# A graph layer on one core: additions of attention in pairs, a division moved from GpSimd to VectorE, and one-hots cut in four

## The reference

```
h = relu(layernorm(x))                       # node stage
h = h @ W.T                                  # 8 heads of 32
enc = relu(edge_attr @ edge_W.T + edge_b)
alpha = leaky(h[src].a_src + h[dst].a_dst + sum(enc * h[dst]))   # per edge and head
attn = softmax of alpha over the edges of one dst
x = x + segment_sum(h[src] * attn, dst) + bias
h = relu(layernorm(x))                       # second dense stage ("mid")
y1 = relu(batch_norm(gcn_conv(h, W1)))       # conv: sum over edges of table[src], scaled
y2 = relu(batch_norm(gcn_conv(y1, W2)))
x = x + relu(concat(h, y1, y2) @ Wfc + bfc)
```

## Time and profile before

| | us |
|---|---|
| median of 3 runs | 6951.39 (6950.96 to 6955.41) |
| profiled execution, its span | 6959.5 |
| of it: units 0 to 127, node stage 127 to 314 | 314 |
| attention, 314 to 2614 | 2300 |
| second dense stage, 2614 to 2808 | 194 |
| first convolution, 2808 to 4814 | 2006 |
| turn, 4814 to 4890 | 76 |
| second convolution, 4890 to 6872 | 1982 |
| last turn, 6872 to 6959 | 87 |

### The profile page before, as it was taken

The page is one execution under the profiler, slowest core; times in us unless marked ns, Lnnn a source line. Parts: engine busy times, 40 slices in busy tenths (PEclk is TensorE's granted clock), DMA queues, the critical chain, the costliest instruction groups (busy, mean ns, idle before and its releaser), DMA issues. The chain is left out here.

```text
span 6959.5 us, 113181 instructions
## 1 busy us (share of the span) xinstructions
PE 4805.8 (69%) x27409; PEld 3529.7 (51%) x27410; DVE 3523.0 (51%) x8745; ACT 2073.8 (30%) x5831; POOL 4908.5 (71%) x4806
## 2 busy tenths in 40 slices
PE   2699999999999994555555555556666666666655
PEld 1466666666666664344444444445544544444443
DVE  6688888888888888222222222223222222222224
ACT  3567777777777774000000000001000000000001
POOL 1777777776776756677777777774677777777775
PEclk9899999999999997555555555555555555555555
DMA  6777776777776655211111111111211111111115
GB/s 207 250 210 211 210 215 207 211 212 212 212 213 210 209 175 158 82 52 52 51 52 52 51 52 51 52 51 43 53 33 34 34 33 34 34 34 33 33 26 161
DMA packets 515795, 783.25 MB, mean 113 GB/s; under 512 B 143367, under 2 KB 392452, under 8 KB 514956
## 3 DMA queue, kind: packets, MB, share of 16 engines
q0 software_dynamic: 176176, 377.82, 21.0%
q1 hardware_dynamic: 303390, 369.82, 16.6%
q10 hardware_dynamic: 35758, 30.37, 1.4%
HBM read 695.07 MB, written 82.51 MB: 112 GB/s over the span
## 5 line engine op out<-in xcount | busy, mean ns | idle before, releaser
L1690 POOL DMA_INDIRECT c_g<-conv_table,c_idx x3128 | 3010.6, 962 | 1128.3 <-issue 952.9
L1767 PE MATMUL c_sums<-c_g,acc 128*128 x7040 | 1976.1, 441 | 1714.2 <-SPq L1653 1077.4
L1767 PEld LDWEIGHTS c_sums<-c_g,acc 128*128 128x128 f32 x7040 | 1626.4, 322 | 2220.1 <-issue 2210.1
L1002 POOL DMA_INDIRECT acc<-gat_table,ga_idx x1564 | 1615.8, 1033 | 653.0 <-issue 458.2
L1731 DVE TENSOR_TENSOR acc<-acc,c_sums 128x128 f32 (+1 forms) x1760 | 448.5, 255 | 2838.1 <-PE c_sums L1767 2821.7
L1386 PE MATMUL ga_sums<-ga_wg,ga_S 128*128 128x265 f32 x3520 | 999.3, 406 | 7.1 <-DVE ga_wg L1260 6.0
L1336 PE MATMUL ga_dstp<-ga_oht,ga_h 128*128 128x256 bf16 x5280 | 729.9, 275 | 76.0 <-DVE ga_prod L1181 69.7
L1386 PEld LDWEIGHTS ga_sums<-ga_wg,ga_S 128*128 128x128 f32 x3520 | 610.4, 193 | 171.4 <-issue 65.3
L1336 PEld LDWEIGHTS ga_dstp<-ga_oht,ga_h 128*128 128x128 bf16 x5280 | 505.7, 98 | 344.4 <-DVE ga_prod L1181 130.1
L1181 DVE SCALAR_TENSOR_TENSOR ga_prod<-acc,ga_a_dst,ga_dstp 128x512 f32<-128x512 f32 x880 | 645.0, 733 | 8.0 <-issue 6.7
L1077 ACT ACTIVATE ga_S<-iota_row,ga_dcol 128x128 f32<-128x128 f32 x1760 | 605.0, 392 | 73.5 <-issue 70.6
(11 more groups left out here) (253 smaller groups left out, 3731.5 us busy)
## 6 DMA issues: line engine op xcount, KB each, us to landing
ga_h<-h_parts SPq DMA_DIRECT2D x880, 192.0 KB
ga_dl<-dl_rows SPq DMA_DIRECT2D x110, 512.0 KB
c_g<-conv_table,c_idx POOLq DMA_INDIRECT x3128, 2.5
acc<-gat_table,ga_idx POOLq DMA_INDIRECT x1564
h_parts<-h_split SPq DMA_DIRECT2D x14, 1344.0 KB, 5.2
gat_table<-h_out SPq DMA_DIRECT2D x14, 952.0 KB
x_rows<-md_x SPq DMA_DIRECT2D x14, 896.0 KB, 7.1
fc_x<-x_rows ACTq DMA_DIRECT2D x98, 128.0 KB
```

What stands on the lines that cost most here:

```text
L1002: pool.indirect_dma_start(G[:, (v * PC + j) * HROW:(v * PC + j + 1) * HROW], None, gat_table, bass.IndirectOffsetOnAxis(idx[:, c:c + 1], 0 ...
L1690: pool.indirect_dma_start(G[:, c % (2 * SLOTS), :], None, table, bass.IndirectOffsetOnAxis(idx[:, c:c + 1], 0)).then_inc(rows_in[c // 2 % ...
L1767: last = nc.tensor.matmul(sums[:, b % R, 0:width], S[:, u * CH + 2 * b + j, :], flat[:, bass.ds(slots[b] * (2 * width) + j * width, width) ...
```

## The change

Five edits:

1. PE's `slot` in attention goes by steps of two. In each: two additions, then `lines`, `carries`, or `factors` with `turn_back` (now ahead of the quanta), then two quanta, then two dots. DVE, ACT and POOL keep their order there.
2. Rows of counts are loaded into registers as the low 16-bit halves of the same words (`low_halves`).
3. The multiplication of POOL in the second dense stage becomes `share` on DVE: for the first group behind the first reciprocal, for group g+1 at the start of `pre(g)`. POOL keeps the addition of the bias.
4. In `dense_phase` scale and shift are written straight into the tiles that are kept, without the two copies and without the wait for the ReLUs of two groups before; and ACT copies tiles 0 to 5 of a group to `md_hT` instead of 1, 3 and 5.
5. A convolution's one-hots are made by four operations with one tensor input and a scalar per partition, 128 columns each, instead of one of 512 with two tensor inputs.

```diff
--- before.py
+++ after.py
@@ -97,6 +98,12 @@
 def spread(ap, dims):
 
     return AP(ap.tensor, ap.offset, [list(ap.ap[0])] + [list(d) for d in dims])
+
+
+def low_halves(tab):
+
+    halves = tab.bitcast(U16)
+    return AP(halves.tensor, halves.offset, [list(halves.ap[0]), [2, tab.shape[-1]]])
 
 
 def gnn(nc, A, out):
@@ -454,8 +461,9 @@
     mv = sb(ctx, f"{name}_mv", [P, GT, 2])
     var = sb(ctx, f"{name}_var", [P, GT])
     sd = sb(ctx, f"{name}_sd", [P, GT])
-    rstd = [sb(ctx, f"{name}_rstd{u}", [P, GT]) for u in range(2)]
-    shift = [sb(ctx, f"{name}_shift{u}", [P, GT]) for u in range(2)]
+    if keep is None:
+        keep = [sb(ctx, f"{name}_{n}", [P, TILES]) for n in ("rstd", "shift")]
+    rstd, shift = ([t[:, g * GT:(g + 1) * GT] for g in range(GROUPS)] for t in keep)
     if tp is None:
         tp = ps(ctx, f"{name}_tp", [P, NT, 512])
     op = [ps(ctx, f"{name}_op{r}", [P, 512]) for r in range(NO)]
@@ -525,16 +533,10 @@
                 nc.vector.tensor_scalar(var[:, :], mv[:, :, 1], EPS, None, ALU.add).then_inc(s_var, 1)
 
             def normal(g):
-                u = g % 2
                 dve.wait_ge(s_sd, g + 1)
-                if g >= 2:
-                    dve.wait_ge(relu_done, GT * (g - 1))
-                link(nc.vector.reciprocal(rstd[u][:, :], sd[:, :]))
-                nc.vector.scalar_tensor_tensor(shift[u][:, :], mv[:, :, 0], -1.0, rstd[u][:, :], ALU.mult, ALU.mult).then_inc(s_norm, 1)
+                link(nc.vector.reciprocal(rstd[g], sd[:, :]))
+                nc.vector.scalar_tensor_tensor(shift[g], mv[:, :, 0], -1.0, rstd[g], ALU.mult, ALU.mult).then_inc(s_norm, 1)
                 dve.wait_ge(s_norm, g + 1)
-                if keep:
-                    nc.vector.tensor_copy(keep[0][:, g * GT:(g + 1) * GT], rstd[u][:, :])
-                    nc.vector.tensor_copy(keep[1][:, g * GT:(g + 1) * GT], shift[u][:, :])
 
             def copy(n):
                 dve.wait_ge(turn_done, n + 1)
@@ -573,8 +575,8 @@
                     act.wait_ge(s_norm, g + 1)
                 if g >= NH:
                     act.wait_ge(turn_done, GT * (g - NH) + a + 1)
-                nc.scalar.activation(hn[g % NH][:, a, :], xg[g % NX][:, a, :], ACT.Relu, bias=shift[g % 2][:, a:a + 1],
-                                     scale=rstd[g % 2][:, a:a + 1]).then_inc(relu_done, 1)
+                nc.scalar.activation(hn[g % NH][:, a, :], xg[g % NX][:, a, :], ACT.Relu, bias=shift[g][:, a:a + 1],
+                                     scale=rstd[g][:, a:a + 1]).then_inc(relu_done, 1)
 
             def copy(n):
                 act.wait_ge(turn_done, n + 1)
@@ -1050,7 +1052,7 @@
                         act.wait_ge(raw_done, t)
                     take_waits(act, held)
                     return (registers(row_tab[u][0:1, 0, :], mybir.EngineType.Activation, 0, NS - 1),
-                            registers(row_tab[u][0:1, 1, :], mybir.EngineType.Activation, READY + 1, READY + 1 + UNITS // PB))
+                            registers(low_halves(row_tab[u][0:1, 1, :]), mybir.EngineType.Activation, READY + 1, READY + 1 + UNITS // PB))
 
                 def source(regs, b):
 
@@ -1389,25 +1391,27 @@
                 def slot(x, a, b, c, tail, more):
 
                     t, m, v = x.at(), x.at(-1), x.odd(-1)
-                    for k in range(QS):
-                        if k == 0 and tail:
-                            add(x.at(-3), UL - 1)
-                        if k and c:
-                            add(x.at(-2), k - 1)
+                    for k in range(0, QS, 2):
+                        for n in (k - 2, k - 1):
+                            if k == 0 and tail:
+                                add(x.at(-3), UL + n)
+                            if k and c:
+                                add(x.at(-2), n)
                         if b and k == 2:
                             lines(m)
                         if b and k == 4:
                             carries(m, v)
-                        if a and k < QS - 2:
-                            quantum(t, k + 2)
-                        if more and k >= QS - 2:
-                            quantum(t + 1, k + 2 - QS)
-                        if a and k % 2:
-                            dot(t, k - 1)
-                            dot(t, k)
                         if b and k == 6:
                             factors(m)
                             turn_back(m)
+                        for q in (k + 2, k + 3):
+                            if a and q < QS:
+                                quantum(t, q)
+                            if more and q >= QS:
+                                quantum(t + 1, q - QS)
+                        if a:
+                            dot(t, k)
+                            dot(t, k + 1)
                     if a:
                         close(x)
 
@@ -1453,8 +1457,11 @@
             link(nc.vector.tensor_scalar(dens(0, 1), dens(0, 1), 1e-10, None, ALU.max))
             nc.vector.reciprocal(dens(0, 1), dens(0, 1)).then_inc(den_ready, 1)
             nc.vector.tensor_scalar(dinv[:, :], acc[:, :, S0], 1.0, None, ALU.add).then_inc(deg_ready, 1)
+            dve.wait_ge(den_ready, 1)
+            share(dve, 0)
             link(nc.vector.tensor_scalar(dens(1, GROUPS), dens(1, GROUPS), 1e-10, None, ALU.max))
             nc.vector.reciprocal(dens(1, GROUPS), dens(1, GROUPS)).then_inc(den_ready, 1)
+            dve.wait_ge(den_ready, 2)
             dve.wait_ge(root_ready, 1)
             link(nc.vector.reciprocal(dinv[:, :], dinv[:, :]))
             dve.sem_inc(dinv_ready, 1)
@@ -1471,14 +1478,17 @@
             pool.wait_ge(s_w, 32)
             for g in range(GROUPS):
                 heads = columns(g)[:, :, :, 1:HCOLS]
-                den = columns(g)[:, :, :, 0:1]
-                if g < 2:
-                    pool.wait_ge(den_ready, g + 1)
-                nc.gpsimd.tensor_tensor(heads, heads, spread(den, [[WROW, GT], [HCOLS, HEADS], [0, HDIM]]), ALU.mult).then_inc(scaled, 1)
                 pool.wait_ge(scaled, g + 1)
                 nc.gpsimd.tensor_tensor(heads, heads, spread(bias[:, :], [[0, GT], [HDIM, HEADS], [1, HDIM]]), ALU.add).then_inc(attended, 1)
 
+        def share(dve, g):
+
+            heads, den = columns(g)[:, :, :, 1:HCOLS], columns(g)[:, :, :, 0:1]
+            nc.vector.tensor_tensor(heads, heads, spread(den, [[WROW, GT], [HCOLS, HEADS], [0, HDIM]]), ALU.mult).then_inc(scaled, 1)
+
         def pre(dve, g, xg):
+            if g + 1 < GROUPS:
+                share(dve, g + 1)
             dve.wait_ge(attended, g + 1)
             x = xg[:, :, :].rearrange("p t (h d) -> p t h d", d=HDIM)
             nc.vector.tensor_tensor(x, x, columns(g)[:, :, :, 1:HCOLS], ALU.add).then_inc(pre_done, 1)
@@ -1507,7 +1517,7 @@
             nc.scalar.activation(acc1[:, t, :], op[:, 0:F1], ACT.Copy, scale=dinv[:, t:t + 1]).then_inc(done, 1)
 
         dense_phase(nc, sb, ps, sem, held, const, "md", ctx, A["x"], NODES, [w1[:, 0, :], w1[:, 1, :]], F1,
-                    lambda pe: pe.wait_ge(s_w, 32), pre=pre, keep=x1_norm, finish_act=finish_act, by_act=(1, 3, 5), hold=hold, at_end=at_end,
+                    lambda pe: pe.wait_ge(s_w, 32), pre=pre, keep=x1_norm, finish_act=finish_act, by_act=(0, 1, 2, 3, 4, 5), hold=hold, at_end=at_end,
                     reloaded=reloaded, act_before=act_before, sync_before=sync_before, dve_before=dve_before, pool=attend)
 
 
@@ -1600,7 +1610,7 @@
 
 
     _, regs = nc.values_load_multi_w_load_instructions(
-        row, engines=[eng], min_val=USED, max_val=USED + UNITS,
+        low_halves(row), engines=[eng], min_val=USED, max_val=USED + UNITS,
         skip_runtime_bounds_check_because="unit numbers are clamped where they are worked out")
     return regs
 
@@ -1714,8 +1724,10 @@
                     dve.wait_ge(dcol_ready, m + 1)
 
                 def onehots(u, b):
-                    nc.vector.tensor_tensor(S[:, u * CH + 2 * b:u * CH + 2 * b + 4, :], spread(iota_row[:, :], [[0, 4], [1, P]]),
-                                            spread(dcol[u][:, 2 * b:2 * b + 4], [[1, 4], [0, P]]), ALU.is_equal).then_inc(onehot_done, 2)
+                    for c in range(2 * b, 2 * b + 4):
+                        last = nc.vector.tensor_scalar(S[:, u * CH + c, :], iota_row[:, :], dcol[u][:, c:c + 1], None, ALU.is_equal)
+                        if c % 2:
+                            last.then_inc(onehot_done, 1)
 
                 def iteration(m, u, i, fc, more):
                     _, tiles = nc.values_load_multi_w_load_instructions(
@@ -1756,7 +1768,7 @@
                         slot_row[0:1, bass.ds(m * UL, UL)], engines=[mybir.EngineType.PE], min_val=0, max_val=NB * PB - 1,
                         skip_runtime_bounds_check_because="pair numbers are taken modulo the slots where they are worked out")
                     _, needs = nc.values_load_multi_w_load_instructions(
```

(3 more changed lines are left out.)

## The result

The changed kernel takes 7030.8 us in the median of 4 runs (7029.4 to 7033.8), before 6951.2; ratio 1.012, 95% interval 1.0105 to 1.0134. That is slower by 80, inside the range on record (6960 to 7110) and 8 under the forecast of 7039. The parts of the sum fit less well than the sum, and one that was put at nothing measured 52. The stages show where to look.

A forecast was written before the change was run, and what follows sets the result against it. It took PE to bound attention, DVE and POOL blocking each other the second dense stage, and POOL's gathers the convolutions; 6951.4 + 140 (order) − 31 (dense) − 21 (one-hots), loads 0, = 7039 us, range 6960 to 7110.

The forecast's parts named there:

- Attention's order: PE's paired order in attention: DVE's product comes late, net 1.29 us a round over 108 rounds, +140 us (+110 to +175).
- the chain: Attention: first addition of a pair, DVE's flush, weigh and product, then PE's dst; ready at 2.97 us against 2.99.
- k = 0, 2 and 4: Pairs of units in an attention round; product forecast late by 0.76, 0.05 and 1.17 us there.
- Rival B: Attention: the pairs are not late, stalls stay as today; 6899 us, chance 0.08.
- D: Attention: half the stall, only k = 0 and half of k = 4 late; +70, 6969 us, chance 0.07.
- The loads: 16-bit register loads on queues with slack: same number and fields, 0 us, bounds −5 and +5.
- The dense stage: Second dense stage: POOL's multiplication moved to DVE, a group falls from 11.7 to 9.7 us; −31 (−20 to −42).
- rival E: Second dense stage: POOL's addition gets in first, 13.4 us a group; +21 instead of −31, 7091 us, chance 0.07.
- my 8.46: Second dense stage before the change: 8.46 us for a group after POOL's last work, the start of the 9.7 estimate.
- The one-hots: Convolutions: four one-input operations leave 26 of 47 us of gather delay; −21 us, bounds −33 and +15.
- Rival C: Convolutions: one-input one-hots hold POOL's port as a train; +96 instead of −21, 7156 us (spread evenly 7286), chance 0.10.

The follow-up runs named there:

- the base: The kernel before with only the 16-bit register loads (of the row counts) made: 6999.8 us, ratio 1.0074.
- the other edits: The changed kernel with PE's old order put back in attention: 6918.6 us, ratio 0.9955.
- leaky early: The order-only kernel with DVE's leaky and scan moved ahead of the flush at unit 0: 7069.0 us, ratio 1.0171.
- order-only kernel: Also called the order alone: the base with only PE's new order in attention added: 7118.5 us, ratio 1.0247.
- the kernel with 16 halves: The base with ACT's and PE's loads of counts taking 16 contiguous 16-bit halves, the even ones used: 7293.8 us, ratio 1.0493.

## Why the prediction held, term by term

- **Attention's order: right in mechanism, the size left open.** Forecast +140 on the kernel before; measured +119 on the base and +112 beside the other edits, with PE's wait for the product at 144 us in the window where about 170 was named. The places and the waits are those of the chain: 0.76, 0.05 and 1.17 forecast at k = 0, 2 and 4, and 0.70, 0.16 and 1.01 found. Rival B, that the pairs are not late, and D, that they are half as late, are out: leaky early took away just the wait that it should. The order alone also takes in some of the base's own waits for ACT (72 us of them in the window there, 48 in the order-only kernel), so its price without the 16-bit loads may be higher; that was not run.
- **The loads: the step that failed.** The prediction said "The number of register loads is the same, and they fetch the same fields", and put the term at 0. Number and fields are the same, and a load of eight counts takes 1.3 us longer on PE and about 1.2 on ACT. On PE, at 1.93, it is hidden, as the prediction said of queues with slack, and nothing shows a loss from SP's. ACT has slack too, 27% of its time, but the addition came only 0.38 behind the one-hot, and the hole grew by 1.16, from 0.68 to 1.84: +52. What I left out was to bound the duration of an operation that the trace did not show, on each queue, against that queue's lead and not its average.
- **The dense stage: right in mechanism, mis-sized.** Forecast −31, found −46. POOL's addition takes 5.4 behind DVE's (forecast 5.7), never ahead of it, so rival E is out. A group of DVE takes 8.57 (2843.91 to 2852.48 in the timeline below), sometimes 9.14 with a wait for a DMA, where I took 9.7. The timeline of DVE after:

```profile
2843.91 2.03 DVE L1487 TENSOR_TENSOR acc<-acc 128x1792 f32<-128x1792 f32 x1 [0.47 <-DMA md_x<-in_x]
2845.85 2.02 DVE L1494 TENSOR_TENSOR md_x<-md_x,acc 128x1792 f32<-128x1792 f32 x1
...
2850.93 0.49 DVE L533 TENSOR_SCALAR md_var<-md_mv 128x7 f32<-128x7 f32 x1
2851.70 0.20 DVE L537 RECIPROCAL x_scale<-md_sd 128x7 f32<-128x7 f32 x1 [0.27 <-ACT md_sd L571]
...
2852.48 2.02 DVE L1487 TENSOR_TENSOR acc<-acc 128x1792 f32<-128x1792 f32 x1
```

  What is left of the blocking is 0.3 at the variance (0.49, where it takes 0.17 undisturbed). ACT's square root, for which the undisturbed group before waited 1.30, is nearly ready: 0.27. That wait was in my 8.46 and I took no credit for it.
- **The one-hots: right in mechanism, mis-sized.** Forecast −21, found −36 alone, and −36 in the profiles of the changed kernel against the base (4009.1 for 4045.1). Of the term, what remains of the delay was put at 26 between 14 and 62; the mean of 949 over the median of 945 gives 4 × 3128 = 13, the lower bound. The median is 945 in the base too, so that it fell by 2 from the kernel before is not the one-hots' doing. POOL's and DVE's timelines after, one train:

```profile
3507.14 0.98 POOL L1700 DMA_INDIRECT c_g<-conv_table,c_idx  x1 [0.30 <-issue]
```

```profile
3506.63 0.87 DVE L1728 TENSOR_SCALAR acc<-iota_row,c_dcol 128x128 f32<-128x128 f32 x4
```

  The train covers the moment at which the gather reads its indices, 3507.14 + 0.13, and runs on to 3507.50; the gather is late by 0.03 only. Rival C, a port held as a train, would make that 0.23 and is out. The Trainium skill (SBUF — State Buffer, "Who interferes with whom") has a one-input operation in a 2-port mode hold the shared pair for the whole instruction. These runs disagree with a holding as long as the recorded duration. An operation is recorded with 0.28 in the median, the train covers the moment of reading in 735 gathers of the changed kernel, and these have a mean of 959 and none is over 1033: at most 0.09 late. That agrees with a holding of about 0.1, the work that the prediction estimated for 128 columns. Whether these operations run in such a mode, and which part of the recorded time holds the port, no run here separates.

So the forecast of 7039 was nearer than its terms, and that is luck: the order was put 21 too high against the base, the loads 52 too low, the gain of the dense stage 15 and that of the one-hots 15 too small. The errors cancel, and the 8 that is left says nothing of how good the terms were.

## What to carry to other kernels

An edit that only changes the type in which a few numbers are loaded needs a duration of its own, and a long operation on a queue is to be held against the lead of that queue over the next engine, not against its average slack: the same loads cost 52 us in one piece and nothing that shows in three. When work is grouped in twos, write out for each engine what the second of the group now stands behind; two orders with the same matmuls, both with the 16-bit loads, lay 198 us apart (7118.5 and 7316.9). A wait of the matmul engine can also cost twice: behind one of 2.47 in the round shown PE ran at the lower clock. And where two engines share a port, ask which operand forms need it before asking how long an operation is.

## What the runs showed of the hardware

A load of registers from 16-bit elements took 0.23 us an element (on PE 1.93 for 8 that lie two apart, 3.80 for 16 in a row), where 8 words of 32 bits took 0.59. On POOL the load of its 16-bit list took 1.82 where the 32-bit one took 1.83, so it isn't so on every engine. Four fp32 one-input operations of 128 columns on DVE, recorded with 0.28 each, followed one another at 0.20 and left 4 ns on a mean gather beside them, at most 0.09 on a single one; four with two inputs left 12, one of 512 columns 15 (mean over median). PE's granted clock was 1.00 from 700 to 2500 in the changed kernel, and 0.94 over attention in the kernel with 16 halves, where in the round shown it was 0.50 for 3 us behind a wait of 2.47.
